# Attention moments of a graph layer: v stationary and float32 features moving, queries projected by columns, bias as three bf16 rows

## The reference

```python
qkv = (x @ Wqkv.T + bqkv).reshape(B, N, 3, H, D)
q, k, v = ...                      # each (B, H, N, D)
q = q * scale
v1 = jnp.concatenate([ones, v], axis=-1)            # 33 columns
qn = _normalize(q) * (scale * temperature)
kn = _normalize(k) * scale
vN = v1 / N
kv_mod = jnp.einsum('bhni,bhnj,bhne->bhije', kn, kn, vN)
kv = jnp.einsum('bhnd,bhne->bhde', kn, vN)
vsum = jnp.sum(vN, axis=-2)[:, :, None, :]
y = A * jnp.einsum('bhni,bhnj,bhije->bhne', qn, qn, kv_mod) + scale ** 2 * Bc * jnp.einsum('bhnd,bhde->bhne', qn, kv) + scale ** 4 * Cc * vsum
```

## Time and profile before

| | us |
|---|---|
| median of 3 runs | 3880.06 |
| lowest and highest | 3876.38, 3881.92 |
| the profiled execution, its own time | 3884.5 |
| its span in the trace | 3882.8 |
| granted TensorE clock, mean over the span | 0.841 of 2.4 GHz |
| busy: PE, DVE, POOL, ACT | 76%, 51%, 44%, 22% |
| moments stage, from its first instruction to the next stage's first | 135.1 to 605.0 |

### The profile page before, as it was taken

How to read it: one execution, slowest core, us unless ns; L and a number is a source line. 1 busy time by engine, 2 the same in 40 slices (tenths; PEclk the granted TensorE clock), 3 DMA queues, 4 the chain that set the end, 5 groups by cost and what they waited for, 6 DMA issues and landing times. The chain is left out here.

```text
span 3882.8 us, 61285 instructions
## 1 busy us (share of the span) xinstructions
PE 2948.0 (76%) x19834; PEld 1946.5 (50%) x19834; DVE 1994.2 (51%) x3409; ACT 836.0 (22%) x1454; POOL 1700.8 (44%) x1616
## 2 busy tenths in 40 slices
PE   1466666888895999994899997599999150599990
PEld 1244543555553565652565664355555040488880
DVE  4599997777424565654465554455554641000002
ACT  1233333444300111121111112011111030232220
POOL 0144443444205777742777770677773004000005
PEclk6677777888666999997899999699999655799995
DMA  1200000000035444533355441444442322411103
GB/s 39 75 0 0 0 0 1 0 0 0 3 124 184 143 151 144 153 116 109 117 153 157 150 148 49 149 125 124 122 127 74 73 78 90 152 60 63 60 19 102
DMA packets 182014, 333.29 MB, mean 86 GB/s; under 512 B 27487, under 2 KB 134908, under 8 KB 181213
## 3 DMA queue, kind: packets, MB, share of 16 engines
q0 software_dynamic: 61968, 167.46, 14.7%
q1 hardware_dynamic: 119884, 163.82, 12.8%
HBM read 245.01 MB, written 86.17 MB: 85 GB/s over the span
## 5 line engine op out<-in xcount | busy, mean ns | idle before, releaser
L1155 POOL DMA_INDIRECT g_ring<-h_rows,idx x786 | 795.8, 1012 | 454.5 <-issue 222.7
L1003 PE MATMUL g_pagg<-g_onehot,g_ring 128*128 128x192 f16 x4716 | 486.3, 257 | 210.1 <-DMA g_ring<-h_rows,idx 149.7
L1003 PEld LDWEIGHTS g_pagg<-g_onehot,g_ring 128*128 128x128 f16 x4716 | 420.0, 102 | 383.8 <-issue 216.1
L1155 POOL DMA_INDIRECT g_ring<-xn_rows,idx x393 | 396.2, 1008 | 293.4 <-PEq L1198 174.0
L1072 DVE TENSOR_TENSOR g_agg<-g_agg,g_pagg 128x384 f32 x393 | 217.7, 554 | 417.8 <-PE g_pagg L1003 390.9
L1079 DVE SCALAR_TENSOR_TENSOR g_onehot<-iota_keys,g_shift,keys 128x576 f16<-128x576 f16 x393 | 319.2, 813 | 0.6 <-DVE g_at L1221 0.6
L1628 DVE TENSOR_TENSOR f_ys<-f_p,f_b 128x256 f32<-128x256 f32 x58 | 24.6, 425 | 533.9 <-PE f_p L1603 533.9
L715 POOL TENSOR_TENSOR mq_Fl<-mq_F,mq_Fh 128x448 f16<-128x448 f32 x168 | 191.4, 1166 | 233.6 <-ACT mq_Fh L700 229.9
L1649 POOL DMA_INDIRECT fc_y<-slots_out,slot_of x56 | 52.0, 929 | 509.7 <-PEq L1643 492.9
L502 PE MATMUL mk_pm<-mk_v,mk_Fh 112*128 112x33 bf16 x3360 | 159.8, 189 | 149.4 <-issue 149.4
L502 PEld LDWEIGHTS mk_pm<-mk_v,mk_Fh 112*128 112x128 f16 x3360 | 157.4, 104 | 160.2 <-issue 160.0
(11 more groups left out here) (277 smaller groups left out, 5146.3 us busy)
## 6 DMA issues: line engine op xcount, KB each, us to landing
h_cols<-g_hn SPq DMA_DIRECT2D x42, 448.0 KB
h_rows<-g_rowb SPq DMA_DIRECT2D x42, 448.0 KB
g_hT<-h_cols SPq DMA_DIRECT2D x42, 448.0 KB, 7.4
f_w<-in_L_ffn_W SPq DMA_DIRECT2D x16, 1024.0 KB
g_ring<-h_rows,idx POOLq DMA_INDIRECT x786, 2.8
g_hT<-xn_cols SPq DMA_DIRECT2D x21, 448.0 KB, 7.2
slots_in<-fg_none SPq DMA_DIRECT2D x64, 128.0 KB, 1.7
ft_x<-slots_in SPq DMA_DIRECT2D x8, 1024.0 KB
```

Of the source, the lines that this page charges most:

```text
L1003: mm = e.matmul(pg[:, k * TYPES:(k + 1) * TYPES, :].rearrange("p t d -> p (t d)"), ring[:, b % SLABS, c, o:o + P], onehot[:, b % 3, c, :], ...
L1155: e.indirect_dma_start(ring[:, b % SLABS, c, :], None, tables[s], bass.IndirectOffsetOnAxis(ap=idx[:, q:q + 1], axis=0)).then_inc(landed[b ...
```

## The change

All of it is in `mix_moments`, which is now written out for all tiles instead of looping.

**Queries by columns.** Before the tiles, 14 units (7 groups of 448 nodes x 2 halves of the channels) project q with the weights stationary and `xnT` moving, so that q comes out with channels on partitions. ACT writes q plus bias squared (`qs`) and plain (`qc`), PE sums the squares by heads with a block matrix of ones, ACT takes the root, DVE makes the maximum, the reciprocal and the product over 128 x 448, and ACT and DVE write the two parts of `qT`. The transposes of `qn` are gone.

**Moments.** The features stay float32 and move; v (112 x 33, float32) is stationary. Heads go in pairs: the even head writes PSUM partitions 0 to 32, the odd head 64 to 96, of the same columns (the program gives these matmuls an array tile of 128 x 64 at columns 0 and 64). `Fh`, `Fl`, the bf16 parts of v and all POOL work in the loop are gone. DVE makes the features of two heads with one instruction. After the last tile the sums, 33 x 577 for each head, are copied to SBUF and turned by 40 matmuls with the identity.

**Bias.** The bias of k and v is split in three bf16 rows at the start; one bf16 matmul of three rows adds it.

**Order.** `project(i + 2)` stands on PE behind the moments of tile `i`; on DVE `squares(i + 1)` stands ahead of `features(i)`.

```diff
             @block.tensor
-                def body(e, i, b, more):
-                    e.wait_ge(S["qn"], i + 1)
-                    e.wait_ge(S["q_lo"], i + 1)
-                    for k in range(KC):
-                        mm = e.transpose(pqt[:, k, :], qn[:, k * P:(k + 1) * P], ident[0:PT, 0:PT])
-                    mm.then_inc(S["qt"], 1)
-                    if more:
-                        project(e, i + 1, 1 - b)
-                    e.wait_ge(S["f_lo"], i + 1)
-                    e.wait_ge(S["f_lo_pool"], i + 2)
-                    e.wait_ge(S["v_parts"], i + 2)
-                    for u in range(HEADS * FCH):
-                        h, c, j = u // FCH, u % FCH, u % 15
-                        for f, parts in ((Fh[b], v[b]), (Fl[b], v[b][0:2])):
-                            for part in parts:
-                                mm = e.matmul(pm[u // 15][:, j * VD:(j + 1) * VD], f[:, h, c * P:(c + 1) * P], part[:, h, :],
-                                              start=False, stop=False, skip_group_check=True)
-                    mm.then_inc(S["mm"], 1)
+                def project(i):
+                    if i >= 2:
+                        e.wait_ge(S["sq"], i - 1)
+                        e.wait_ge(S["v"], i - 1)
+                        e.wait_ge(S["ext"], i - 1)
+                    for k in range(KC):
+                        e.matmul(pkv[i % 2][:, :], xnT[:, k, i * PT:(i + 1) * PT], w[:, k, C:3 * C], start=(k == 0), stop=False)
+                    e.matmul(pkv[i % 2][:, :], ones3[:, :], bias3[:, :], start=False, stop=True).then_inc(S["kv"], 1)
...
+                for n in range(QT):
+                    query(n)
+                    if n:
+                        norm(n - 1)
+                norm(QT - 1)
+                e.wait_ge(S["biased"], 1)
+                project(0)
+                project(1)
+                e.wait_ge(S["q_root"], QT)
+                for i in range(TILES):
+                    e.wait_ge(S["v"], i + 1)
+                    e.wait_ge(S["linear"], i + 1)
+                    e.wait_ge(S["feat"], i + 1)
+                    for h in range(0, HEADS, 2):
+                        for half in range(2):
+                            for d in range(2):
+                                a, b = pieces(h + d)[half]
+                                f = a - column(h + d, 0)
+                                mm = e.matmul(pm[a // 512][64 * d:64 * d + VD, a % 512:a % 512 + b - a], vf[i % 2][:, h + d, :], F[i % 2][:, h + d, f:f + b - a],
+                                              start=(i == 0 and a % 512 == 0), stop=(i == TILES - 1), skip_group_check=True)
+                    mm.then_inc(S["mm"], 1)
+                    if i + 2 < TILES:
+                        project(i + 2)
...
             @block.scalar
+                def spread(i):
+                    e.wait_ge(S["kv"], i + 1)
+                    if i >= 2:
+                        e.wait_ge(S["ss"], i - 1)
+                        e.wait_ge(S["mm"], i - 1)
+                    e.activation(sq[i % 2][:, :], pkv[i % 2][:, 0:C], ACT.Square).then_inc(S["sq"], 1)
...
+                for i in range(TILES):
+                    if i + 1 < TILES:
+                        spread(i + 1)
+                    copies(i)
+                    if i + 1 < TILES:
+                        scale(i + 1)
...
             @block.vector
+                def query(n):
...
+                    e.wait_ge(S["q_root"], n + 1)
+                    q(e.tensor_scalar(qr[n % 2][:, :], qr[n % 2][:, :], 1e-12 / (4 * SC * SC), None, ALU.max))
+                    q(e.reciprocal(qr[n % 2][:, :], qr[n % 2][:, :]))
...
+                    e.tensor_tensor(qn[n % 2][:, :], qc[n % 2][:, :], qr[n % 2][:, :], ALU.mult).then_inc(S["q_new"], 1)
...
+                for i in range(TILES):
+                    if i + 1 < TILES:
+                        squares(i + 1)
+                    features(i, 0)
+                    features(i, 2)
+                    if i + 1 < TILES:
+                        inverse(i + 1)
+                    features(i, 4)
+                    if i + 1 < TILES:
+                        extend(i + 1)
+                    features(i, 6)
```

More of the change, by code:

```diff
@@ L384, in mix_moments @@
[L384 to L408, removed]
+        mask = sb("mask", [PT, 1])
@@ new lines, in mix_moments @@
+        vf = [sb(f"vf{b}", [PT, HEADS, VD]) for b in range(2)]
+        sums = sb("sums", [P, 5 * 512])
+        pm = [ps(f"pm{i}", [P, 512]) for i in range(5)]
+        pkv = [ps(f"pkv{b}", [PT, 2 * C]) for b in range(2)]
+        S = {n: sem(f"mk_{n}") for n in ("in", "zero", "mask", "set", "biased", "bq_sum", "bq", "q_sum", "q_out", "q_norm", "q_root", "q_dve", "q_new", "q_hi", "q_lo",
+                                         "kv", "sq", "v", "ss", "root", "small", "ext", "wrap", "linear", "feat", "mm", "sums", "turned", "out")}
@@ new lines, in query @@
+                def query(n):
+                    m = n % KC
+                    e.wait_ge(S["q_sum"], n + 1)
+                    if n >= 2:
+                        e.wait_ge(S["q_norm"], n - 1)
+                        e.wait_ge(S["q_new"], n - 1)
+                    e.activation(qs[n % 2][:, :], pm[n % 2][:, 0:GW], ACT.Square, bias=bq[:, m:m + 1]).then_inc(S["q_out"], 1)
+                    e.activation(qc[n % 2][:, :], pm[n % 2][:, 0:GW], ACT.Identity, bias=bq[:, m:m + 1]).then_inc(S["q_out"], 1)
@@ new lines, in _ @@
+                e.wait_ge(S["bq"], 1)
+                for n in range(QT + 2):
+                    if n < QT:
+                        query(n)
+                    if 0 < n <= QT:
+                        root(n - 1)
+                    if n > 1:
+                        high(n - 2)
+                spread(0)
+                scale(0)
+                for i in range(TILES):
[4 more added lines that the diff above has]
+                        scale(i + 1)
@@ L508, in _ @@
+                for m in range(5):
+                    e.wait_ge(S["mm"], TILES)
+                    e.activation(sums[0:VD, m * 512:min((m + 1) * 512, HH * NW)], pm[m][0:VD, 0:min(512, HH * NW - m * 512)], ACT.Copy).then_inc(S["sums"], 1)
             @block.vector
             def _(e):
-                step = counted(e, S["vset"], 0)
-                step(e.memset(zero[:, :], 0.0))
-                step(e.memset(one[:, :], 1.0))
-                for f in Fh + Fl:
-                    step(e.memset(f[:, :, NF:FP], 0.0))
@@ L515, in _ @@
-                for f in Fh:
-                    step(e.memset(f[:, :, NF:NF + 1], 1.0))
-                e.wait_ge(S["in"], 16 * 3)
+                step = counted(e, S["small"], 0)
+                for hh in range(P // HD):
+                    step(e.tensor_reduce(block_sum[:, hh:hh + 1], ident[:, hh * HD:(hh + 1) * HD], AX.X, ALU.add))
+                step(e.tensor_copy(block_ones[:, :, :], block_sum[:, :].unsqueeze(2).to_broadcast([P, P // HD, HD])))
+                e.sem_inc(S["set"], 1)
@@ new lines, in _ @@
+                e.wait_ge(S["bq_sum"], 1)
+                e.tensor_copy(bq[:, :], pm[4][:, 0:KC]).then_inc(S["bq"], 1)
+                e.memset(sums[:, :], 0.0)
+                e.memset(one[:, :, :], 1.0)
+                e.memset(ones3[:, :], 1.0)
+                for b in range(2):
+                    e.memset(vf[b][:, :, 0:1], 1.0 / N)
+                    e.memset(F[b][:, :, NF:NW], 1.0)
+                e.wait_ge(S["in"], 16 * 4)
+                step(e.tensor_copy(part[0][:, :], bkv[:, :]))
@@ new lines, in _ @@
+                step(e.tensor_tensor(left[:, :], bkv[:, :], part[0][:, :], ALU.subtract))
+                step(e.tensor_copy(part[1][:, :], left[:, :]))
+                step(e.tensor_tensor(left[:, :], left[:, :], part[1][:, :], ALU.subtract))
+                step(e.tensor_copy(part[2][:, :], left[:, :]))
+                step(e.tensor_scalar(three[:, :], part[0][:, :], ident[0:3, 0:1], None, ALU.mult))
+                step(e.scalar_tensor_tensor(out=three[:, :], in0=part[1][:, :], scalar=ident[0:3, 1:2], in1=three[:, :], op0=ALU.mult, op1=ALU.add))
@@ L520, in _ @@
+                step(e.scalar_tensor_tensor(out=bias3[:, :], in0=part[2][:, :], scalar=ident[0:3, 2:3], in1=three[:, :], op0=ALU.mult, op1=ALU.add))
+                e.sem_inc(S["biased"], 1)
                 step(e.tensor_tensor(tsq[:, :], temp[:, :], temp[:, :], ALU.mult))
@@ new lines, in _ @@
+                for n in range(QT + 1):
+                    if n < QT:
+                        query(n)
+                    if n:
+                        low(n - 1)
+                squares(0)
+                inverse(0)
+                extend(0)
+                for i in range(TILES):
[9 more added lines that the diff above has]
+                    features(i, 6)
@@ L569, in _ @@
+                for m in range(5):
+                    e.wait_ge(S["mm"], TILES)
```

(3 more changed lines are left out.)

232 lines of the change are left out of this document (121 added, 111 removed).

## The result

| | before | after |
|---|---|---|
| median of the runs, us | 3880.99 | 3947.56 |
| lowest and highest | 3876.38, 3884.83 (4 runs) | 3945.68, 3954.63 (4 runs) |
| ratio after to before | | 1.0175, 95% interval 1.0158 to 1.0193 |
| the profiled execution, its own time | 3884.5 | 3948.36 |
| its span | 3882.8 | 3946.4 |

The change makes the kernel slower by 66.6 us in the medians, 1.75%. The prediction was 3948 us.

What follows compares the result with a forecast made beforehand. DVE's 15.65 us a tile was taken as the bound. Moments from 237 us, 26 periods of 15.5, 10.3 for the last two tiles and 13 of tail made the stage 68 us longer: 3948 us, range 3905 to 4075.

Steps and rivals of the forecast that it cites:

- The bound and the new order: Tile loop: DVE's 15.65 us a tile falls to 6.2, but PE and DVE take turns, so the period is 15.5.
- H: Tile loop: the way from the projection's end on PE to the features' end on DVE, 7.0 us.
- P: PE's projection of one tile: 1.94 us, made of 1.73 for float32 columns and 0.21 for bf16 columns.
- M: PE's moments of one tile: 3.89 us with head pairs fully overlapped, 7.78 us one after another.
- rival B: Tile moments on PE: the pairs run one after another, period 19.4 us, time 4057 us; chance 0.30.
- The clock: Tile loop on PE: each burst starts at half clock for 5 us after the pause and loses 2.5 us.
- rival D: Tile loop: PE keeps full clock through the waits, period 13.0 us, time 3880 us; chance 0.07.
- The reciprocal: Query units on DVE: 448 elements take 2.95 us at 6.25 ns an element, in a unit of 5.8 us.
- rival C: Query units: the reciprocal costs as little as other operations, 33 us less, time 3915 us; chance 0.08.
- The tail: Behind the tiles: copies of sums and 40 turns on PE, net 13 us, 8 to 18.
- A: Tile moments on PE: the pairs overlap, time 3948 us, stated range 3920 to 3985; chance 0.50.

Runs made afterwards that it cites:

- three runs on the locks: Changed kernel with projection ahead of the moments and v held three times: 3729.6 us; only projection ahead: 3905.8 us; only v held three times: 3952.3 us.
- the kernel with both locks open: Changed kernel with tile i + 2's projection ahead of tile i's moments, and v held three times: 3729.6 us.

## Why the prediction was right

- **The bound and the new order.** Read right, and it is the reason for the sign. DVE's work in a tile falls from 15.65 to 6.05 us (6.2 were reckoned) and the period stays, since the order makes PE and DVE take turns. The three runs on the locks show two waits that keep the turns. The prediction named only the first, the projection behind the moments; by its working, moving the projection would have ended the turns, and the run that did only this still took 3905.8 us. ACT's wait for the moments, because v is held twice, does not show in the changed kernel, as the other wait is longer, so the number did not suffer from it.
- **H.** Predicted 7.0 us from P's end to the next moments, measured 6.74 (460.23 to 466.97). The feature instructions take 1.24 us each as reckoned (two of them 2.49).
- **M and P, rival B.** Full overlap of the pairs was taken, with no row to show it. The order without pairs costs 2.9 us a tile, and at full clock 6.97 against 4.02 us. The page "TensorEngine Tiling (Array Packing)" of the Trainium skill, section "Tiling Modes", says that tiles work independently and can run in parallel: the trace agrees, with 4.02 us where half of 7.78 is 3.89. B would have been 4057; the run without pairs gave 4039. P was put too low: 1.94 us, measured 2.32 (457.91 to 460.23), 0.42 of it the row of the bf16 matmul, which was put at 0.21, a price that no row of before shows.
- **The clock, rival D.** Predicted 5 us at half clock in each burst, so 2.5 us lost. In the burst shown it is 5.8 us (451.05 to 456.85), in the next one 3.5, where the moments take 5.74 us instead of 6.86; the mean loss is 2.3. M + P was put at 8.5 us and is 9.18 and 8.06 in turn, 8.62 on the mean: the low P, the 0.2 us for starts and the high price of the clock nearly cancel. D was excluded for the right reason, the pause; when the pause was filled the period was 13.08, where the text said 13.0. Its price was low, 3880 against 3894: that stage ended 11.9 us behind the one of before instead of level with it, 6 us by the dearer tail and 5 by the periods, 3 of these by the first one, still at half clock.
- **The reciprocal, rival C.** 2.95 us by the slope of two rows, measured 2954 ns fourteen times; the unit was put at 5.8 us and is 5.78 (154.83 to 160.61). By the page "VectorE: DVE Perf Modes" of the Trainium skill, section "First, the fixed hardware budget", the estimate was 3.7 us. The trace disagrees, with 2.95 us, and the measurement decides for the rows' slope of 6.25 ns an element.
- **The tail: the mis-sized term.** Put at 13 us net, it is 17 (26.5 us from 646.38 to 672.9, against 9.5 before). One us of that is a slip: 3.0 + 12.3 - 1.9 + 0.6 is 14. The step that failed is the price of the 40 turns, 12.3 us from a float32 weight load of 154 ns; the group of the changed kernel, and three of its windows, read

```profile
L488 PEld LDWEIGHTS mk_pm<-ident,mk_sums 128*128 128x128 f32 x80 | 15.2, 300 | 3.4 <-DVE mk_sums L662 3.4
649.00:651.00 2.00, 1.71 (x16) 1.71 (x16) 0.23 (x1) 0.00 (x0) 0.00 (x0) 1.00 0.00 0
651.00:652.00 1.00, 1.00 (x9) 1.00 (x8) 0.00 (x0) 0.00 (x0) 0.00 (x0) 0.70 0.09 16
652.00:664.00 12.00, 12.00 (x58) 12.00 (x58) 1.35 (x2) 0.00 (x0) 0.00 (x0) 0.50 0.00 0
```

  that is 15.4 us for 80 records. At full clock a record comes every 0.11 us (16 in 1.71), at half clock every 0.21 (58 in 12), and three quarters of them fall to the half clock. The 154 ns of the earlier trace rows are the mean length of a record in bursts of the old kernel, neither of the two prices. The clock falls at 651.4, two us into the turns, and stays at 0.50 to their end though PE has no gap; in the kernel with both locks open it is the same (1.00 until 425.1, then 0.50). The prediction counted no half clock here, and no run shows what keeps it down.
- **What the exactness hides.** The tiles ended 4 us earlier than predicted (first moments 1 us, periods 3) and the tail was 4 us longer; these cancel. The stage was 67.9 us longer where 68 was said, but the total of a single execution moves by as much as these errors in stages that nothing touched. So the mechanism was right and a part of the exactness is luck. Three smaller slips changed nothing: A's range, worked out from its own bounds, is 3930 to 3973, not 3920 to 3985; two hand-overs are 0.1 us, so a guess of 0.2 does not lie between nothing and them; and the float32 burst at 139.6 stays at half clock for 5.0 us, not 4.3.

## What to carry to other kernels

When a change makes an engine's work cheaper, write down for one period who stands behind whom in each engine's order, with the work of the next tile in it; busy shares of two engines that add up to nearly 100%, together with waits of each for the other in the list, are the sign here that they take turns. A look-ahead counts only from the place at which the consumer waits: the projection was issued two tiles early, but behind the moments that waited for the features, and a second wait, on a buffer held twice instead of three times, kept the turns even when the projection was moved. So when one wait is removed, look for the next that would take its place. The turns cost TensorE twice here, since each pause of 6.7 us also took its clock, 2.3 us a tile.

## What the runs showed of the hardware

- Two float32 matmuls with 33 stationary columns, at array columns 0 and 64, run at once if they are neighbours in PE's order: 16 of them took 4.02 us at full clock, 6.97 in an order with one such place.
- TensorE's granted clock was 1.00 until 463.7 and 0.50 from there on after a burst that ended at 460.2; before the change it fell 1.2 us after a burst that ended at 553.0. With 5.4 us of unused matmuls in a pause of 6.7 us it stayed at 1.00.
- VectorE's reciprocal of float32 takes 2.95 us for 448 elements a partition, against 0.39 for a maximum over the same: 6.25 ns an element.
- Float32 matmuls of 33 columns with 128 stationary columns, each with its weight load, came every 0.11 us a record at full clock and every 0.21 at half clock: 40 of them, 80 records, took 15.4 us, and 13 of these were at 0.50 though PE had no gap.
